# Moving the last merge of the denominators, and the output projection that hangs on it, behind other work of the first half

## What is computed

```
x = x + attention0(groupnorm(x))          # softmax attention, 4 heads of 32, all 4096 tokens against all
t = x as tokens
t = t + attention1(layernorm(t))          # linear attention: softmax over q's head channels, over k's tokens,
                                          # context = k.v, then a norm over the whole image
t = t + experts(layernorm(t))             # 8 experts of 128x128, the best 2 by router, weighted
```

## Time and profile before

| | us |
|---|---|
| median of three runs | 3132.67 |
| lowest, highest | 3129.98, 3133.64 |
| the profiled execution, its own time | 3128.74 |
| its span, first to last instruction | 3126.9 |
| TensorE busy in it | 2902.8 (93%) |
| VectorE busy | 2573.8 (82%) |
| ScalarE busy | 2434.3 (78%) |
| GpSimd (POOL) busy | 698.4 (22%) |

### The profile page before, as it was taken

The page is one execution under the profiler, slowest core; times in us unless marked ns, Lnnn a source line. Parts: engine busy times, 40 slices in busy tenths (PEclk is TensorE's granted clock), DMA queues, the critical chain, the costliest instruction groups (busy, mean ns, idle before and its releaser), DMA issues.

```text
span 3126.9 us, 62137 instructions
## 1 busy us (share of the span) xinstructions
PE 2902.8 (93%) x20368; PEld 1024.5 (33%) x20368; DVE 2573.8 (82%) x3652; ACT 2434.3 (78%) x3196; POOL 698.4 (22%) x726
## 2 busy tenths in 40 slices
PE   6999999978799999997979999999788999999978
PEld 3222222375322222237532222223743222222474
DVE  4888888878688888887868888888786888888877
ACT  4999999744599999974469999997446999999734
POOL 1112221114212212211421221121152122122115
PEclk8999999989899999998989999999898999999989
DMA  2555555500155565540025556554001555555300
GB/s 84 111 114 109 110 109 108 95 1 16 55 109 109 113 115 111 98 92 1 21 62 110 109 110 115 101 109 82 1 22 41 111 111 111 109 106 111 68 1 28
DMA packets 72168, 257.86 MB, mean 82 GB/s; under 512 B 8160, under 2 KB 10240, under 8 KB 71808
## 3 DMA queue, kind: packets, MB, share of 16 engines
q0 software_dynamic: 64512, 234.91, 39.8%
q1 hardware_dynamic: 7296, 18.51, 1.6%
HBM read 10.12 MB, written 8.39 MB: 6 GB/s over the span
## 4 chain that ended last, share of the span: by engine, by line
PE 77%; issue 10%; DVE 6%; DMA 2%; ACT 2%; POOL 1%; SPq 0%; ACTq 0%; DVEq 0%; POOLq 0%
PE BK L1032 76%; DMA RM<-EA 2%; DVE X L1005 2%; ACT KE L534 1%; POOL KE L457 1%; PE BK L1037 1%; DVE ST L642 1%; ACT PVC L513 1%; DVE X L841 0%; ACT KE L547 0%; ACT XT L552 0%; DVE X L997 0%; DVE RU L635 0%; DVE RU L636 0%; DVE ST L681 0%
## 5 line engine op out<-in xcount | busy, mean ns | idle before, releaser
L812 DVE TENSOR_TENSOR XT<-XT,KE 128x512 f32<-128x512 f32 x1344 | 1567.2, 1225 | 193.5 <-ACT KE L534 193.5
L534 ACT ACTIVATE KE<-BK 128x512 f32<-128x512 f32 (+1 forms) x1536 | 1489.0, 1021 | 152.0 <-PE BK L1032 65.0
L1032 PE MATMUL BK<-Q,K 32*128 32x512 f32 x8192 | 1190.7, 651 | 25.5 <-issue 13.2
L1032 PE MATMUL BK<-KE,V 128*32 128x512 f32 x6144 | 818.5, 606 | 0.0
L416 POOL DMA_DIRECT2D RM<-EA x448 | 392.0, 929 | 1544.4 <-ACT EA L534 748.1
L1032 PEld LDWEIGHTS BK<-Q,K 32*128 32x128 f32 x8192 | 325.9, 185 | 897.9 <-ACT KE L534 636.9
L534 ACT ACTIVATE EA<-BK 128x512 f32<-128x512 f32 (+1 forms) x512 | 496.9, 1025 | 34.7 <-PE BK L1032 6.5
L1032 PEld LDWEIGHTS BK<-KE,V 128*32 128x32 f32 x6144 | 125.5, 108 | 580.4 <-ACT KE L534 503.6
L1032 PE MATMUL BK<-EA,V 128*32 128x512 f32 x2048 | 272.7, 604 | 0.0
L1032 PE MATMUL BK<-WEXP,XT 128*128 128x512 f32 x512 | 236.9, 609 | 16.4 <-DVE X L1005 16.4
L610 ACT ACTIVATE RM<-BK,GT 128x128 f32<-128x128 f32 x512 | 145.9, 368 | 136.0 <-PE BK L1032 136.0
(11 more groups left out here) (153 smaller groups left out, 1883.4 us busy)
## 6 DMA issues: line engine op xcount, KB each, us to landing
RM<-EA POOLq DMA_DIRECT2D x224, 768.0 KB, 6.7
RM<-EA POOLq DMA_DIRECT2D x224, 256.0 KB, 3.3
XN<-in_x SPq DMA_DIRECT2D x16, 512.0 KB, 5.8
out<-X SPq DMA_DIRECT2D x16, 512.0 KB, 2.9
WEXP<-in_L_ffn_expert_w SPq DMA_DIRECT2D x1, 512.0 KB, 6.9
CONST<-in_consts SPq DMA_DIRECT2D x1, 384.0 KB, 5.8
WQKV<-in_L_conv_w_qkv SPq DMA_DIRECT2D x1, 192.0 KB, 2.4
WQKV<-in_L_attn_W_qkv SPq DMA_DIRECT2D x1, 192.0 KB, 6.0
```

The source lines that it names most:

```text
L534: nc.scalar.activation(exps(jt, p), scored(c * T + jt, p).rearrange("p a n -> p (a n)"), ACT.Exp, scale=SCALE0).then_inc(s_exp, 1)
L812: v.tensor_tensor(acc, acc, exps(jt, p), ALU.add).then_inc(s_adds, 1)
L1032: return nc.tensor.matmul(o, lhsT, rhs, start=start, stop=stop, skip_group_check=shared)
```

## The change

On DVE the merge of the last chunk leaves the first half's additions and goes behind the whole of the first half's layer norm. On TensorE the sums go behind the first half's four groups of transposes, and `project(7)` goes behind the first half's values. Nothing is computed in another way, and no instruction is added or dropped.

```diff
                     for c in range(first, first + HCH):
                         onto_x(ready, done, c)
-                        if c == 1 and ready is s_y0:
-                            dve.wait_ge(s_zero, b + 1)
-                            merge(b * NCH + NCH, 1, True)
                         if c > first:
...
                 onto_x_and_normed(s_y0, s_x0, 0)
 
+                dve.wait_ge(s_zero, b + 1)
+                merge(b * NCH + NCH, 1, True)
                 dve.sem_inc(s_smc, 1)
                 reciprocals(b * NCH + NCH, s_sum, SM)
                 onto_x_and_normed(s_y0, s_x0, 1)
...
                 project(3)
-                sums(b * NCH + NCH, 1, SM)
                 project(4)
                 project(5)
...
                     for c in chunks:
                         transposed(0, c)
+                    if half == 0:
+                        sums(b * NCH + NCH, 1, SM)
                     for c in chunks:
                         pe.wait_ge(s_zc, b * (2 * NCH) + c + 1)
                         mm(BK[c], WQKV1[:, C:2 * C], XT[:, c * CH:(c + 1) * CH]).then_inc(s_k1, 1)
-                    if half == 0:
-
-                        pe.wait_ge(s_ot, b * NCH + NCH + 1)
-                        project(7)
                     for c in chunks:
                         pe.wait_ge(s_k1c, b * NCH + c + 1)
                         token_major(c, WQKV1[:, 2 * C:3 * C], s_v1)
+                    if half == 0:
+
+                        pe.wait_ge(s_ot, b * NCH + NCH + 1)
+                        project(7)
```

More of the change, by code:

```diff
@@ L1224, in _ @@
                         mm(BK[c], WQKV1[:, C:2 * C], XT[:, c * CH:(c + 1) * CH]).then_inc(s_k1, 1)
+                    for c in chunks:
+                        pe.wait_ge(s_k1c, b * NCH + c + 1)
+                        token_major(c, WQKV1[:, 2 * C:3 * C], s_v1)
                     if half == 0:
@@ L1228, in _ @@
                         project(7)
-                    for c in chunks:
-                        pe.wait_ge(s_k1c, b * NCH + c + 1)
-                        token_major(c, WQKV1[:, 2 * C:3 * C], s_v1)
                     if half == 0:
```

## The result

| | before | after |
|---|---|---|
| median, us | 3131.32 (4 runs, 3127.79 to 3133.64) | 3149.19 (4 runs, 3147.58 to 3149.84) |
| ratio | | 1.0055, interval 1.0041 to 1.0068 |
| span of the profiled execution | 3126.9 | 3147.8 |
| PE busy | 2902.8 | 2922.1 |

The change makes the kernel 17.9 us slower. 3143.1 was forecast, with a range of 3137.0 to 3149.5: the sign and what bounds the stretch were right, the size was 6 us short, and the median stands at the range's upper end.

What follows compares the result with a forecast made beforehand. DVE was taken to bound the stretch, except where PE's `project(7)` just barely does; 9.24 us for the order plus 1.2 us for the clock, 10.4 us, added to 3132.67 gave 3143.1 us, range 3137 to 3149.5.

Steps and rivals of the forecast that it cites:

- What bounds the stretch: Mixing stage: DVE bounds it, except at chunk 7's addition, where PE's `project(7)` just barely does, by a 0.39 us stop.
- rival C: Second half's keys run at 1.2 GHz for half their length, 1.7 us later: 16 us more, 3149; chance 0.15.
- -2.26 for the merge, +1.00 for the sums, +3.57 for the values: Path to chunk 7's addition: the three moves together delay it by 2.31 us per turn, 9.24 us in four turns.
- The cover of 0.15 us over the merge: Before the sums on PE: the moved merge ends some 0.15 us before PE reaches the sums, so no wait.
- Rival D: Merge comes too late and PE waits before the sums, 0 to 1.26 us per turn: up to 3148; chance 0.05.
- The new gap, 0.3 us per turn: Before the second transposes PE idles some 3.3 us, so they run at 1.2 GHz: 1.2 us in all.
- The tail at zero: Clock in the keys' transposes is dealt anew by the shift: put at zero, some 2 us either way over four turns.
- Rival B: Gap before the keys' transposes shrinks and the clock may stay up, 2.2 us less per turn: 3133; chance 0.12.

Runs made afterwards that it cites:

- Project alone: The code before with only `project(7)` moved behind the first half's values, merge and sums left in place: 3149.14 us, +18.8 (ratio 1.0063).
- The delay alone: The code before with one extra reciprocal of 128x432 numbers on DVE ahead of the addition of chunk 7: 3146.98 us, +16.2 (ratio 1.0045).

## Why the prediction was right, and where its size was off

*What bounds the stretch.* Right. DVE's addition of chunk 7 was the place, and it waits for `project(7)` in every turn after. Project alone moved it by 14.2 us, against 14.3 from the values' length. That the median lies within the range is luck, though. It is 0.3 us inside; as a difference the range ran from 4.3 to 16.8 us over 3132.67, and the change cost 17.9 over a median before of 3131.32. And it lies where rival C put it, 3149, by another sum than C's.

*-2.26 for the merge, +1.00 for the sums, +3.57 for the values.* Right where the clock allows it: 2.21 us in turns 3 and 4, against 2.31. In turns 1 and 2 the 1.00 was mis-sized: the sums took 1.94 us, and the keys behind them 3.92 from 3.60, so the place moved 3.3 to 3.7 us. I had priced the sums at a row in which they run at full speed. In the first turn of the code before, the work right behind the transposes does run at 1.00, but I took that turn for all: in the others the first half's keys take 3.88, 3.83 and 3.77 us instead of 3.60, at a granted clock of 0.92, 0.94 and 0.95, so there the clock comes back only within them. And the change starts these transposes 2.26 us earlier and after a longer gap, so that even the first turn's row was no measure for the new place.

*The cover of 0.15 us over the merge* held: PE never waits there. In turn 1 the merge ends at 621.43 and the sums start at 621.79, the slower transposes giving it time; in turn 3 it is 2184.47 and 2184.52. So in the third turn it held by 0.05 us, not by 0.15. Rival D did not come up; it shows, with 0.45 us, only when the clock is held.

*The new gap, 0.3 us per turn.* It is as long as forecast (3.29 us), and the transposes behind it run at the clock that was forecast (0.50 in the first turn). Its price was too low: between the addition of chunk 7 and the exponential of the keys, the change lost 1.2 us in each of turns 1 and 2 and 0.2 in each of turns 3 and 4, 2.7 us against 1.2. In the first the keys took 4.72 us (3.69 before), and DVE waited for their copies. This is rival C in a smaller form.

*The tail at zero.* This is the step that failed in kind. I wrote that the later passages' clock is dealt anew and put it at zero, with 2 us either way, from the keys' transposes alone. These indeed gave a little back (9.9 us from the exponential to the next queries, against 9.5 to 11.2). The router's passage took 6.4 us more, and I had not priced it: its small matmuls (32 records) take from 4.03 to 7.00 us, a spread that stands in the trace of before too. The delay alone shows that it comes with a mere shift.

*Rival B* (the clock gives the loss back) fell: the gap before the keys' transposes did shrink, from 3.54 to 2.91 us, but that gave back 1.7 us in all where B had 8.8, and the later clock took more.

In the profiled pair the parts are 9.2 (order), 2.2 (sums and first keys slow), 2.7 (second keys), 6.4 (router) and -1.7 (the keys' transposes), together some 19 of 20.9; the rest is spread over the passages between.

The Trainium skill (TensorE: Matmul & The Clock Gate, HAM oscillation — how this bites in real kernels) warns of idle gaps of PE as what brings the low clock back. The runs agree: filling the gaps took 7.6 us off the code before, and brought the change from +17.9 to +4.2.

The router's passage takes 19.3 to 20.2 us, or 22.4. That this goes with the granted clock is shown, and the traces also tell where it is settled: in the second pass over the norm before it (the second group `BK<-AT,EA`, 64 records, 7.31 us when all at full speed). Over the 40 turns of the ten profiled executions whose tail is not filled, a pass of 8.75 to 9.98 us was followed by a passage of 19.3 to 20.2, and one of 10.00 to 10.33 us by 22.4, without exception. In the code before no turn is beyond 9.71, in the change the third and fourth are (10.10 and 10.08). What stays open is why the clock comes back later in that pass in one turn than in another; no run here varies that alone, and the attempt to fill the gaps did not settle it.

## What to carry to other kernels

A step that is moved costs what it costs in its new place: look up the granted clock of that place, in every turn and not in one, before taking its duration from the old one, and price the low clock where the place itself moves. When a stretch is shifted by a few microseconds, price the passages behind it that show two lengths in the trace, since a shift alone can turn them, and a gain at the bound can be lost there as easily as a delay can double. Work taken off the engine that bounds and given to an idle one paid here only together with filling TensorE's gaps.

## What the runs showed of the hardware

- The same eight records of the sums took 1.06 us at a granted clock of 1.00 and 1.94 at 0.50; 32 records of 128x8 took 4.03 us at 0.92 and 6.99 at 0.50.
- Gaps of PE of 1.58 to 1.90 us before the second transposes (the delay alone) left the clock at full for what followed; those of 3.29 us in the change did not in any turn. These are no limits: in the code before, transposes behind a gap of 2.08 us ran at 0.58 (709.9 to 713.2), with matmuls at 0.79 ahead of the gap.
- Ten unread records in the gap before the first transposes of the change ended 0.84 us before the tokens were there, so they held nothing up, and the clock stayed at 1.00. Eight in a later gap of 3.6 us took 5.38.
- A stretch without a break can stay at the low clock: in the code before, 32 records of 128x8 kept PE busy for 6.88 of 6.90 us at 0.50 (2254.6 to 2261.5), and the transposes behind them ran at 0.50 as well.
- POOL added 128x2048 numbers onto as many in 4.69 us, for which DVE takes 2.35.
